# Blocks built on TensorE: the compared numbers kept in PSUM, two banks, and every eviction on ScalarE

## The reference

```python
h = relu(layernorm(x))
# layer 0 (weighted sum of neighbours, two products, row-normalized)
x_neigh = segment_sum(edge_w[:, None] * h[src], dst)
out = h @ w_self.T + x_neigh @ w_neigh.T
x = x + out / max(norm(out), 1e-12)
# layer 1: two graph convolutions (degree-normalized, unweighted counts), 256 -> 128 -> 256
# layer 2: two hops with the weighted, degree-normalized matrix, then h @ W.T + b
# layer 3: two relational layers, msg = relu(xt[edge_type, src] + b), summed by dst
```

## Time and profile before

| | us |
|---|---|
| median of 3 runs | 2842.55 |
| the profiled execution | 2843.29 |
| its span (first to last instruction) | 2841.4 |
| TensorE busy, whole span | 2525.3 |
| VectorE busy | 1327.8 |
| ScalarE busy | 561.7 |
| GpSimd busy | 1726.6 |
| first and last target tile's records taken by VectorE | 106.4 and 681.8 |
| first and last block multiplied | 115.4 and 714.8 |

### The profile page before, as it was taken

How to read it: one execution, slowest core, us unless ns; L and a number is a source line. 1 busy time by engine, 2 the same in 40 slices (tenths; PEclk the granted TensorE clock), 3 DMA queues, 4 the chain that set the end, 5 groups by cost and what they waited for, 6 DMA issues and landing times.

```text
span 2841.4 us, 44073 instructions
## 1 busy us (share of the span) xinstructions
PE 2525.3 (89%) x12873; PEld 2026.6 (71%) x12874; DVE 1327.8 (47%) x2836; ACT 561.7 (20%) x1659; POOL 1726.6 (61%) x1701
## 2 busy tenths in 40 slices
PE   6799999899898999999999997998788879987675
PEld 4598888788798988888777774665555546555454
DVE  7799988797322551111244233444333424433332
ACT  1355555555100000000011112111011121110000
POOL 5788878772067777774000004777777657777776
PEclk9899999999999999999999998999999989998888
DMA  3133333333698779945444434555454545554343
GB/s 98 50 146 149 151 142 128 121 143 140 207 295 281 241 250 349 314 151 158 134 133 150 134 118 135 161 155 154 133 150 148 148 131 160 155 148 113 115 115 100
DMA packets 208107, 454.85 MB, mean 160 GB/s; under 512 B 52672, under 2 KB 141870, under 8 KB 207818
## 3 DMA queue, kind: packets, MB, share of 16 engines
q1 hardware_dynamic: 56004, 257.55, 26.0%
q0 software_dynamic: 66944, 111.48, 14.9%
q10 hardware_dynamic: 84998, 83.76, 8.7%
HBM read 285.85 MB, written 166.80 MB: 159 GB/s over the span
## 4 chain that ended last, share of the span: by engine, by line
PE 54%; POOL 27%; issue 13%; DMA 3%; DVE 2%; ACT 1%; ACTq 1%; PEldq 0%; DVEq 0%; POOLq 0%; PEld 0%; SPq 0%
PE agg L980 29%; POOL edges_bucketed L665 16%; POOL gathered L720 12%; PE agg L1028 10%; PE y L819 10%; PE prod L804 2%; DMA gathered<-table_rel,idx_rel 1%; DMA edges_bucketed<-edges,pos_u 1%; PE agg L884 1%; ACTq L1259 1%; PE turn_ps L789 0%; ACT turned L1079 0%; PE y L860 0%; DMA table_rel<-y_sb 0%; DVE relw L1494 0%
## 5 line engine op out<-in xcount | busy, mean ns | idle before, releaser
L720 POOL DMA_INDIRECT gathered<-table_rel,idx_rel x840 | 810.6, 965 | 696.5 <-ACTq L1259 443.8
L1028 PE MATMUL agg<-gathered,onehot 128*128 x2464 | 617.1, 407 | 137.5 <-SPq L620 81.6
L1028 PEld LDWEIGHTS agg<-gathered,onehot 128*128 128x128 f32 x2464 | 492.0, 204 | 266.5 <-issue 197.2
L665 POOL DMA_INDIRECT edges_bucketed<-edges,pos_u x416 | 507.0, 1219 | 148.1 <-issue 124.0
L980 PE MATMUL agg<-t_sb,stream 128*128 128x128 f32 (+1 forms) x3750 | 562.8, 312 | 14.6 <-issue 7.6
L980 PEld LDWEIGHTS agg<-t_sb,stream 128*128 128x128 f32 x3750 | 526.2, 193 | 48.4 <-issue 14.8
L1794 DVE SCALAR_TENSOR_TENSOR onehot<-iota,keybase,edges 128x256 f32<-128x256 f32 x616 | 278.1, 483 | 592.2 <-PE agg L1028 482.7
L704 POOL DMA_INDIRECT edges_parted<-parted,pos_u x416 | 402.0, 966 | 180.2 <-issue 126.1
L819 PE MATMUL y<-relw,turned 128*128 128x512 f32 x600 | 283.2, 617 | 74.1 <-ACT turned L1094 41.4
L884 PE MATMUL agg<-h_sb,stream 128*128 128x257 f32 x1250 | 338.5, 396 | 0.0
L860 PE MATMUL y<-gathered,relw 128*128 128x128 f32 x1300 | 238.8, 293 | 41.1 <-DVE t_sb L1511 15.2
(11 more groups left out here) (198 smaller groups left out, 1740.3 us busy)
## 6 DMA issues: line engine op xcount, KB each, us to landing
table_rel<-y_sb ACTq DMA_DIRECT2D x200, 256.0 KB, 2.9
stream<-counts_dense SPq DMA_DIRECT2D x50, 832.0 KB
stream<-weights_dense SPq DMA_DIRECT2D x50, 832.0 KB
stream<-counts_dense SPq DMA_DIRECT2D x50, 768.0 KB
stream<-weights_dense SPq DMA_DIRECT2D x50, 768.0 KB
table_rel<-zeros ACTq DMA_DIRECT2D x2, 12800.0 KB, 92.6
weights_dense<-stream SPq DMA_DIRECT2D x25, 832.0 KB, 3.4
counts_dense<-t_sb SPq DMA_DIRECT2D x25, 832.0 KB, 5.2
```

The source lines that it names most:

```text
L665: pool.indirect_dma_start(recs_dram, bass.IndirectOffsetOnAxis(ap=pos_u[0:rows, c:c + 1], axis=0), edges[0:rows, c, :], None).then_inc(s_s ...
L720: pool.indirect_dma_start(gathered[:, slot * D:(slot + 1) * D], None, tables[n], bass.IndirectOffsetOnAxis(ap=idx_rel[:, c:c + 1], axis=0) ...
L1028: mm = pe.matmul(agg[b][:, 0:D], onehot[:, half_ * QUAD + k, :], gathered[:, bass.ds(((q + quads0) & (GQ - 1)) * (QUAD * D) + k * D, D)], ...
```

## The change

- `iota`, the compared row, is copied once into PSUM by a matmul with the identity, after the last ranking product has been read, and L1475 reads it from there (bank `y_ps[3]`).
- The blocks have two banks in place of three, so a group may be built when the group two before it is evicted.
- All evictions are ScalarE's (of 325 evictions, 162 were VectorE's).
- The weighings of the next half come three at a time behind each eviction from the second on, where they were one run of 12 to 14 between the third and the fourth group.
- VectorE makes `dst` directly behind `src`, ahead of the step's small work, and `sum` at the end; it has no evictions.

```diff
-    BANKS = 3
+    BANKS = 2
...
-    def evicted_by(at):
-
-        return at % 2, at // 2 + 1
...
-        built_ps = y_ps[1:]
+        built_ps = y_ps[1:3]
+        iota_ps = y_ps[3][:, 0, 0:P]
...
+            pe.wait_ge(s_picked, RANKED)
+            pe.matmul(iota_ps, ident[:], iota[:], start=True, stop=True).then_inc(s_iota, 1)
+
             pe.wait_ge(s_w, 16 * 8)
...
                 if at >= BANKS:
-                    who, done = evicted_by(at - BANKS)
-                    pe.wait_ge(evicted[who], done)
+                    pe.wait_ge(evicted, at - BANKS + 1)
...
-            def weigh(h):
+            def weigh(h, first, end):
...
-                act.wait_ge(cnt_ready, h + 1)
                 columns = list(range(lo, hi)) + [TILES] * (lo <= t < hi)
-                for j, c in enumerate(columns):
-                    last = nc.scalar.activation(pair_hot[:, h % 2, j, 0, :], pair_hot[:, h % 2, j, 1, :], ACT.Copy,
-                                                scale=recs[:, t % RECS, c, 2:3])
-                last.then_inc(dw_ready, 1)
+                if first == 0:
+                    act.wait_ge(cnt_ready, h + 1)
+                for j in range(first, min(end, len(columns))):
+                    ins = nc.scalar.activation(pair_hot[:, h % 2, j, 0, :], pair_hot[:, h % 2, j, 1, :], ACT.Copy,
+                                               scale=recs[:, t % RECS, columns[j], 2:3])
+                    if j == len(columns) - 1:
+                        ins.then_inc(dw_ready, 1)
...
-            weigh(0)
+            weigh(0, 0, HALF + 1)
...
                 if i < HALVES:
-                    for group in range(len(GROUPS[i % 2])):
-                        if group == 3 and i + 1 < HALVES:
-                            weigh(i + 1)
-                        if evicted_by(groups_until(i) + group)[0] == 0:
-                            evict(i, group)
+                    groups = len(GROUPS[i % 2])
+                    each = -(-(HALF + 1) // (groups - 1))
+                    for group in range(groups):
+                        evict(i, group)
+                        if group >= 1 and i + 1 < HALVES:
+                            weigh(i + 1, (group - 1) * each, group * each)
...
-                        to, iota[:].unsqueeze(1).broadcast_to([P, width, P]),
+                        to, iota_ps.unsqueeze(1).broadcast_to([P, width, P]),
...
                 if ahead:
                     onehots(i + 1, "src")
+                    onehots(i + 1, "dst")
...
-                for group in range(len(GROUPS[i % 2])) if i < HALVES else ():
-                    if evicted_by(groups_until(i) + group)[0] == 1:
-                        evict(i, group)
-                    if ahead and group == 1:
-                        onehots(i + 1, "dst")
-                    if ahead and group == 3:
-                        onehots(i + 1, "sum")
+                if ahead:
+                    onehots(i + 1, "sum")
```

More of the change, by code:

```diff
@@ L312, in build_gnn @@
         built = sem("blocks_built")
-        evicted = [sem("blocks_evicted_by_act"), sem("blocks_evicted_by_dve")]
+        evicted = sem("blocks_evicted")
+        s_iota = sem("iota_in_psum")
         w_stored = [[sem(f"weight_half_stored{k}{j}") for j in range(2)] for k in range(2)]
@@ L565, in _ @@
                     for part in range(2):
-                        for at in range(groups_until(2 * t + part + 1))[-2:]:
-                            who, done = evicted_by(at)
-                            sp.wait_ge(evicted[who], done)
+                        sp.wait_ge(evicted, groups_until(2 * t + part + 1))
                         sp.dma_start(dense(w_dram, t, part), half(t, part)).then_inc(w_stored[t % 2][part], 16)
@@ L880, in sage_sum @@
                 if s in (0, HALF):
-                    for at in range(groups_until(2 * t + (s == HALF) + 1))[-2:]:
-                        who, done = evicted_by(at)
-                        pe.wait_ge(evicted[who], done)
+                    pe.wait_ge(evicted, groups_until(2 * t + (s == HALF) + 1))
                 mm = pe.matmul(sums("sage", t)[:, 0:D + 1], stream[:, t % 2, s * P:(s + 1) * P], table("sage", s),
@@ L1161, in evict @@
                 mine = GROUPS[part][group]
-                if group < 2:
+                if group == 0:
                     if t >= 2:
@@ L1171, in evict @@
                 nc.scalar.copy(c_block[:, columns].rearrange("p (k d) -> p k d", d=P), bank[:, :, P:2 * P]
-                               ).then_inc(evicted[0], 1)
-            weigh(0)
+                               ).then_inc(evicted, 1)
+            weigh(0, 0, HALF + 1)
             for i in range(2 * (TILES - 1) + 10):
@@ L1496, in onehots @@
                                             AXX, ALU.add).then_inc(sum_made, 1)
[L1498 to L1502, removed]
-                    if t >= 2:
-                        dve.wait_ge((half_free, sum_ready)[part], t - 1)
-                        dve.wait_ge(w_stored[t % 2][part], 16 * (t // 2))
-                    if t >= 1:
-                        dve.wait_ge(c_stored[part], 16 * t)
-                dve.wait_ge(built, at + 1)
-                bank, columns = built_ps[at % BANKS][:, 0:len(mine), :], slice(mine[0] * P, (mine[-1] + 1) * P)
-                nc.vector.tensor_copy(stream[:, t % 2, columns].rearrange("p (k d) -> p k d", d=P), bank[:, :, 0:P])
-                nc.vector.tensor_copy(c_block[:, columns].rearrange("p (k d) -> p k d", d=P), bank[:, :, P:2 * P]
-                                      ).then_inc(evicted[1], 1)
+            dve.wait_ge(s_iota, 1)
             for what in ("src", "dst", "sum"):
```

## The result

| | us |
|---|---|
| before, median of 4 runs beside it | 2843.94 |
| after, median of 4 runs | 2879.43 (2876.91 to 2883.81) |
| ratio after / before | 1.013, 95% interval 1.0118 to 1.0142 |
| the profiled execution after, its span | 2877.56, 2875.7 |
| the same of before | 2843.29, 2841.4 |

The change makes the kernel 1.3% slower, 35.5 us by the medians. Between the profiled executions it is 34.3; the stretch from the first block to the next stage grew by 36.0 and the rest of the span shrank by 2. So the question is the build stage, as predicted.

A forecast was written before the change was run, and what follows sets the result against it. TensorE was taken to set the build stage's pace, with VectorE's records sometimes late. 2843.3 + 57.2 new waits - 32.6 old waits and slow clock + 17.6 new slow clock = 2885.5 us, range 2852 to 2908.

The forecast's parts named there:

- The new wait: TensorE's third group of 22 even steps waits 2.38 us, or 2.78 with the spill bucket, for the first eviction: 57.2 us.
- B: Moment when an odd step's last group is built; first eviction seen at B + 7.69 us, needed at B + 5.31.
- The clock: TensorE's slow clock behind new waits: 0 to 22 of them cost 1.6 us more; half taken, +17.6 us.
- The credit: Build-stage waits of TensorE that go, 26.6 us, and their slow clock, 6 us: -32.6 us.
- Sum: Whole kernel: 2843.3 + 57.2 - 32.6 + 17.6 = 2885.5 us, +1.5%.
- Comparison from PSUM at no change: VectorE's comparisons take as long from PSUM as from SBUF; bounds -6 to +4 us.
- GpSimd freed but worth nothing: Row in PSUM may save a scatter up to 1.65 us, worth nothing once records are no longer late.
- The prediction's rival that the scatters would be stopped as before: GpSimd is stopped as before with one operand in PSUM; same time as the forecast, chance counted within its 0.80.
- ScalarE's rate: ScalarE, with all 325 evictions, takes 1.42 us a chunk against TensorE's 1.53 for a group, so it keeps up.
- Rival 3: A ScalarE chunk takes 1.65 us, so TensorE loses 27 us more: 2912 us; chance 0.07.
- Tiles: Build stage: two tiles 25.6 to 26.5 us apart, even from first to last.
- Rival 1: Scatters freed and no new wait in even steps, all 32.6 us go: 2811 us; chance 0.07.

The follow-up runs named there:

- e1: The kernel after, with only the comparisons reading their row from SBUF again; 2882.79 us, 1.0158 of before.
- d2: As d1, but with the comparisons reading their row from SBUF again; 2812.24 us, 0.9902 of before.
- d3: The kernel after, with three banks for blocks and the row in SBUF; 2821.8 us, 0.9941 of before.
- a1: The kernel after, with even steps' target comparison put back behind VectorE's small work; 4207.0 us against 4198.77 for before, 1.0019.
- d1: The kernel after, with ScalarE's degree root and root of even steps moved behind the third group's eviction and weighings; 2799.95 us, 0.9856 of before.
- e2: The kernel before, with two banks for blocks in place of three and nothing else; 2864.11 us, 1.0081 of before.

## Why the prediction was right

Forecast 2885.5 us, range 2852 to 2908, slower with 0.86; measured 2879.4. Step by step:

- **The new wait.** Place, releaser and number were right: the third group of an even step, ScalarE's L1170, 22 times. The size was 2.10 and 2.50 us from start to start against 2.38 and 2.78: 10 x 2.10 + 12 x 2.50 = 51.0 us against 57.2. The 0.28 too much are two terms. The comparison starts 0.04 us after B, not 0.12 (303.27 to 303.31), and the small work takes 309.76 - 306.65 = 3.11 us, not 3.30. Most of the 0.19 is one instruction, L1438, here before, after and in e1, where the row is back in SBUF, with e1's wait:

```profile
317.86 0.33 DVE L1438 TENSOR_SCALAR small<-small 128x2 f32<-128x2 f32 x1
```

```profile
307.20 0.17 DVE L1438 TENSOR_SCALAR small<-small 128x2 f32<-128x2 f32 x1
```

```profile
309.55 0.33 DVE L1438 TENSOR_SCALAR small<-small 128x2 f32<-128x2 f32 x1
```

```profile
313.21 0.49 PE L859 MATMUL y<-gathered,relw 128*128 128x128 f32 x2 [2.12 <-ACT t_sb L1170]
```

  It takes 0.32 or more where a scatter ends 0.03 us behind it. With the row in SBUF the comparisons, by stretching scatters, make that so in every tile (e1 18 times of 18 while scatters run, d2 and d3 21 of 21); with it in PSUM it is chance (after: once among the 22, in the step of the one wait of 2.50 us in place of 2.33). So the row in PSUM shortens the chain by 0.19 us for a wait (1.93 against e1's 2.12), which the prediction did not count; once the scatters are over, e1's waits are after's (2.34 and 2.33). a1 confirms the comparison's 1.67 and 1.87 as terms of their own.
- **The clock.** Summing (1 - granted clock) x 5 us over the stretches of 5 us from 120 us on, up to 735 us before, 750 after and 690 in d1 (behind that, where the blocks run out, all of them slow down), gives 7 us before, 25 after, none in d1. So the term was 25 against a stage without slow clock, not 17.6; the 7 of before stand in the credit. 14 of the 22 waits were followed by a slow stretch, where I took half: 5 of the first ten and 9 of the last twelve, at 25 / 14 = 1.8 us each where I took 1.6 (the row behind it gives 3.00 - 1.53 = 1.47). That they would be about half was a choice between 0 and 22, and no more. One of them (stretch, length, TensorE busy, granted clock, DMA share, GB/s):

```profile
280.00:285.00 5.00, 3.07 (x21) 1.00 0.49 175
285.00:290.00 5.00, 5.00 (x25) 0.66 0.03 2
290.00:295.00 5.00, 5.00 (x32) 1.00 0.22 79
```

- **The credit.** 32.6 us forecast. d1, which has no wait left but the stage's first ones, shows what it was: its stage is 40.7 us shorter than before's. 26.6 + 7.1 of it are the waits and the clock as I read them. Of the other 7, some 4 are what a wait takes beyond its idle time (2.10 from start to start for 1.93 idle: 0.17 for each of 23 waits, an estimate from that step) and 0.8 the first waits of the stage (2.0 us in place of 2.9); the rest is open. The reason was right too: in e1 the records are on time with the scatters colliding, and in e2 with nothing done for GpSimd at all.
- **Sum.** Measured stage: 51 + 25 - 40.7 = +35, against +36.0 read directly and +42.2 forecast. The three errors are -6, +7 and -8: the first two cancel, which is luck, since nothing ties them, and the sum is off by the third.
- **Comparison from PSUM at no change**: 1.76 and 1.75 us for 1536 elements (rows above) against 1.75. The Trainium skill, "VectorE: DVE Perf Modes", TRN2 errata, would by an estimate from its fixed cycles have had it 65 ns longer; the two rows do not agree with that.
- **GpSimd freed but worth nothing**: right for this kernel as far as late records go, which e1 has none of either. Beside that the row is worth a few microseconds through L1438: e1 waits 52.4 us in place of 49.2, has 16 slow stretches in place of 14 and a stage 6.0 us longer, near the noise of the whole time. As a general word on the edit it is wrong: in d1 it is worth 12.3 us. The prediction's rival that the scatters would be stopped as before is refuted: 966 ns against 1219, and the second of the two sentences cited from the Trainium skill's "SBUF — State Buffer", "Who interferes with whom" (descriptor generation not hit by a VectorE instruction with two SBUF inputs) is contradicted by d2 beside d1, which differ in that operand alone: 1143 against 963 ns.
- **ScalarE's rate**: 1.42 us for a chunk when it catches up (from the second group's first copy, 310.51, to the third's, 311.93); no waits in odd steps. Rival 3 did not occur.
- **Tiles**: 25.6 to 26.5 us apart and even from first to last was forecast; they are 25.8 (234.43 to 415.27, seven tiles) and later 26.4 (442.43 to 706.89, ten), but not even: 24.9 and 26.5 in turns at first, later mostly 26.9 with a 25.3 in between, because the slow clock comes behind some waits and not behind others.
- **Rival 1** (2811 us, if nothing new waited) is what d1 built: 2800. The forecast had priced the version that repairs the change within 11 us.

The version that beats both kernels is d1: one move of two small ScalarE operations, 1.4% faster than before and 2.8% faster than after (2799.95 / 2879.43, not measured together). From before to d1 in the runs made together: the order of work on ScalarE and VectorE with three banks -17 us (d3), two banks with evictions first -10 more (d2; the two edits were not separated there), the row in PSUM -12 (d1).

## What to carry to other kernels

When a buffer is taken away, do not compare averages: write down when the release is seen in the worst step and when the next user would naturally come, and look at what stands ahead of the release in its engine's queue. Here two small operations that waited for another engine stood there, and an order whose waits sum to 17 us with three banks (d3) cost 78 us with two, clock and all (after against d1, 0.0274 of 2840). An edit's worth depends on what is last: the row in PSUM gave little while TensorE waited elsewhere (3 to 8 us, near the noise) and 12 us once it did not, and a producer's pace for a tile, counted over a long stretch, against the consumer's tells which. How large its lead is at the start belongs to the account: d3 falls behind too and is never late.

## What the runs showed of the hardware that I had not expected

- e2 waits four times in two tiles (from 314 to 345 us 1.89, 1.12, 0.33 and 0.69 us) and its clock stays at 1.00 in both stretches (TensorE busy 91.6 of 100 us); after, with one wait of 1.93 us for a tile and 92.2 busy, is at 0.97. The length of a wait and the busy share alone do not say whether the clock drops, and in the kernel after waits of the same length differ in it; what decides is open.

```profile
300.00:400.00 100.00, 91.63 (x594) 81.50 (x593) 85.78 (x154) 55.45 (x188) 79.58 (x68) 1.00 0.35 132
475.00:675.00 200.00, 182.82 (x1181) 162.12 (x1180) 170.68 (x308) 110.41 (x376) 142.36 (x120) 1.00 0.36 136
```

- The granted clock gives part of the cure for nothing: d1 removed 51 us of waits and gained 76.7 in the stage against after. d3's 22 waits of 0.3 to 1.0 us were followed by no slow stretch.
- A small VectorE instruction (L1438, 128x2) takes 0.33 us in place of 0.17 where an indirect DMA of GpSimd ends 0.03 us behind it. Comparisons that read SBUF alone bring the two together in every tile, and it stood in the chain that TensorE waited for.
